# Four patch banks, direct loads of the rest weights, throw-away matmuls, and scatter rows normalised in their own chunk

## Chip, core and metric

One core of a Trainium2 chip runs the whole program. The metric is the device time in microseconds of one execution. Matrix products run on TensorE (PE; PEld is its weight load), element work on VectorE (DVE), ScalarE (ACT) and GpSimd (POOL); SyncE (SP) only issues DMAs.

## What is computed

32 images of 3x96x96 are cut into 6x6 patches of 16 pixels, with four copies shifted by 8 pixels: 36 patches of 3840 features. They are layer-normed and projected to 192 features, and 128 text tokens are appended: 164 tokens a batch. Then, with `ln` for a layer norm without weights,

```
xn = (patches - mu) * rsqrt(var + 1e-5) * ln_gamma + ln_beta;  h = concat(xn @ W.T + b, txt)
x  = ln(h);  k, v, gate = of batch 0 alone;  q of every batch
fw(t+1) = 0.95 * fw(t) + 0.1 * gate(t) * outer(k(t), v(t));  r(t) = q(t) @ fw(t)
h  = h + x + r @ w_out.T
x  = ln(h);  xf = rms_norm(x) * norm_w;  probs = softmax(xf @ router_w.T)
y  = sum over the top 2 of 8 experts e:  probs[e] * (silu(xf @ g[e].T) * (xf @ u[e].T)) @ d[e].T
out = h + x + y
```

## The kernel before

**Layout.** Four tokens of all 32 batches make a tile of 128 rows: 41 tiles, of which 9 hold patch tokens. `hres` holds all of them. The recurrence is rewritten in chunks of 16 tokens (4 tiles, 11 chunks, the last of one tile): a chunk reads a state for what lies in the past and a masked score matrix for the present.

**Patches.** `patch(p)` (nine, L687) does 24 matmuls into bank `p % 2` and waits for the read-out of patch p-2. On ScalarE `squares(p + 1)` sums squares of an image band, then the root of patch p is taken; there are two band buffers, so bands 2 and 3 are loaded when the squares of their predecessors are done (L380). On VectorE `patch_out(p)` (L1003) forms the variance, reads the bank into `tmp`, waits for the root and writes the tokens. Between them lie the text tiles' statistics (`stats1`, `scale1`) and normalisation (`add_norm`).

**Between.** Behind the last patch, TensorE projects keys and values of batch 0 (`project`, L719), multiplies them by query and output weights (`text_kv`, L728), picks batch 0's patch tokens with selection matrices (L766 to L769), computes gates (L776), repeats the projections for the first 48 tokens and multiplies those (`head_kv`, L739). ScalarE copies the keys out, VectorE the values (`vals`, L1091).

**Attention, chunk c.** Each engine runs its own list in order; semaphores join them. TensorE (L849): `turn(c+1, 0)` transposes two tiles of the next chunk into bank 1; `past` and `present` of tiles 0 and 1; `turn(c+1, 1)`, which needs bank 1 read out; `past` and `present` of tiles 2 and 3; `state`, `rows(c+2)`, `scores(c+1)`. VectorE (L1220): units of weights (`low`), `residual`, router `sums`, top-2 `picks`, `stats_2`, `mask(c+1)`, `places` (the row of each token in its expert's region), `low`, `scale2`. ScalarE:

```
for c in range(CHUNKS):            # L586
    xT_out(c + 1, 0); high(...); xT_out(c + 1, 1)
    norm2(c - 1)                   # waits for scale2(c - 1); writes the scatter rows xf
    state_out(c + 1); high(...); rows(c + 2)
    add_norm2(c - 1); std2(c)      # waits for stats_2(c)
```

GpSimd scatters each tile of `xf` twice to the regions of its two experts in DRAM (`scatter`, L648), eight indirect DMAs a full chunk; there are three `xf` buffers.

**Expert weights.** Each f32 weight is kept as a rounded high part and the remainder. `high(n)` on ScalarE writes the first, `low(n)` on VectorE the second; a `unit` is a fourth of the eight down matrices' block, or a piece of one expert's gate and up weights: the first 128 input rows as one unit, the last 64 as two, staged through a ring of three buffers that SP reloads as they come free (L388 to L393). 28 units are spread over 22 half-chunks by `turn_units`.

**Experts.** When all tokens are counted, SP clears the tails of the regions (L397), VectorE makes a table of 89 slots of 128 rows, and a pipeline over the slots loads rows (L414), transposes them, multiplies, and stores results (L666). A last stage gathers and adds (L1310).

## Time and profile before

| | us |
|---|---|
| median of 3 runs | 653.4 |
| the runs | 644.21, 653.4, 655.39 |
| the profiled execution, its own time | 646.63 |
| its span | 644.8 |
| busy PE / DVE / ACT / POOL | 508.8 / 366.3 / 282.9 / 185.8 |
| granted TensorE clock, mean share | 0.881 |

The span runs from the first to the last instruction; the execution's own time has 1.8 us around it. Busy PE is time with a matmul listed. A granted clock of 1 is 2.4 GHz, 0.5 is 1.2 GHz. "Idle before" is the time that an engine waited just before an instruction and what released it.

### The profile page before, as it was taken

How to read it: one execution, taken by the hardware profiler on the slowest of the kernel's cores; microseconds unless marked ns; L12 is line 12 of the kernel's file. 1: busy time of each engine (PE TensorE's matmuls, PEld its weight loads, DVE VectorE, ACT ScalarE, POOL GpSimd, SP SyncE). 2: the span in 40 equal slices, each digit the busy share in tenths (PEclk: the TensorE clock that was granted, in tenths of full speed). 3: DMA queues.
4: the chain of work that ended last, by engine and by line, in shares of the span. 5: the costliest groups of instructions: out<-in, count | busy, mean ns of one | idle time of the engine just before them, and what ended most of it. 6: DMA issues, size and time to landing. Idle time of an engine off the chain costs nothing.

```text
span 644.8 us, 12710 instructions
## 1 busy us (share of the span) xinstructions
PE 508.8 (79%) x3128; PEld 474.7 (74%) x3129; DVE 366.3 (57%) x1254; ACT 282.9 (44%) x702; POOL 185.8 (29%) x270
## 2 busy tenths in 40 slices
PE   5998689999767837750699999999999999998000
PEld 2897689878555726540699999999999999998000
DVE  3546457217747635576355655666665556655297
ACT  0364673426556516552344444444444444444100
POOL 0000000000736654456033333333333333334100
PEclk9999999659969878765699999999999999999555
DMA  8972022710212322223122222222222222221795
GB/s 361 429 315 98 2 98 88 256 38 1 87 51 87 100 74 68 70 80 112 46 74 74 72 72 72 72 75 75 79 72 72 72 72 72 72 80 45 253 370 140
DMA packets 55579, 71.62 MB, mean 111 GB/s; under 512 B 18961, under 2 KB 50258, under 8 KB 54018
## 3 DMA queue, kind: packets, MB, share of 16 engines
q1 hardware_dynamic: 41408, 48.12, 23.6%
q0 software_dynamic: 8208, 16.95, 7.4%
q10 hardware_dynamic: 5938, 6.26, 2.8%
q8 instruction: 11, 0.18, 0.1%
q14 instruction: 14, 0.11, 0.1%
HBM read 49.43 MB, written 21.86 MB: 111 GB/s over the span
## 4 chain that ended last, share of the span: by engine, by line
PE 56%; DVE 21%; ACT 6%; another core or an unknown queue 5%; DMA 4%; issue 4%; SPq 2%; ACTq 1%; POOL 0%; DVEq 0%; POOLq 0%
PE bank L921 5%; PE bank L917 5%; PE bank L919 5%; PE bank L920 5%; PE bank L918 5%; PE bank L928 4%; DVE hres L1310 4%; PE bank L937 4%; PE pair L937 4%; DMA band<-in_bands 3%; PE pair L906 3%; ACT sqjunk L447 3%; PE pair L822 3%; PE bank L698 2%
## 5 line engine op out<-in xcount | busy, mean ns | idle before, releaser
L654 POOL DMA_INDIRECT disp<-xf,posu x82 | 80.7, 984 | 220.0 <-ACT xf L557 193.8
L666 POOL DMA_INDIRECT ydram<-ysb,dnow x89 | 87.3, 981 | 69.4 <-POOL dnow L663 66.4
L1275 DVE TENSOR_TENSOR hh<-sg,bank 128x384 f32<-128x384 f32 x89 | 49.3, 554 | 95.1 <-ACT sg L614 93.9
L614 ACT ACTIVATE sg<-bank 128x384 f32<-128x384 f32 x89 | 43.7, 491 | 113.2 <-PE bank L921 113.2
L698 PE MATMUL bank<-wcT,imgT 128*128 128x193 f32 x432 | 74.2, 332 | 10.8 <-DVE tmp L1015 10.8
L698 PEld LDWEIGHTS bank<-wcT,imgT 128*128 128x128 f32 x432 | 72.2, 192 | 12.3 <-DVE tmp L1015 7.7
L917 PE MATMUL bank<-wa,xh 128*128 x178 | 68.1, 383 | 0.0
L919 PE MATMUL bank<-wa,xl 128*128 x178 | 60.5, 340 | 0.0
L921 PE MATMUL bank<-wa,xl 128*128 x178 | 60.5, 340 | 0.0
L920 PE MATMUL bank<-wa,xh 128*128 x178 | 60.5, 340 | 0.0
L918 PE MATMUL bank<-wa,xh 128*128 x178 | 60.1, 338 | 0.0
L822 PE MATMUL pair<-nst,xT 96*128 96x208 f32 x164 | 44.1, 399 | 19.7 <-ACT nst L537 9.7
L663 POOL COPY dnow<-dest 128x1 uint32 (+1 forms) x89 | 16.5, 186 | 123.0 <-DVE ysb L1285 123.0
L822 PEld LDWEIGHTS pair<-nst,xT 96*128 96x128 f32 x164 | 34.3, 227 | 21.6 <-ACT nst L537 10.1
L1278 DVE TENSOR_TENSOR htl<-bank,hth 128x384 fp32r<-128x384 f32 x89 | 49.0, 550 | 0.9 <-ACT hth L617 0.9
L906 PE MATMUL pair<-ident,xs 128*128 128x128 f32 x178 | 34.8, 277 | 18.6 <-DMA xs<-disp 18.6
L937 PE MATMUL pair<-wd,hth 128*128 x135 | 44.8, 381 | 0.4 <-DVE htl L1278 0.4
L928 PE MATMUL bank<-ident,hh 128*128 128x128 f32 x267 | 43.6, 272 | 0.6 <-DVE htl L1278 0.6
L937 PE MATMUL bank<-wd,hth 128*128 x132 | 43.8, 381 | 0.0
L617 ACT CAST hth<-bank 128x384 fp32r<-128x384 f32 x89 | 42.4, 476 | 0.8 <-PE bank L928 0.8
L826 PE MATMUL pair<-crow,sm 128*128 128x200 f32 x82 | 26.6, 412 | 19.8 <-DVE sm L1122 16.2
L611 ACT CAST xh<-pair 128x256 fp32r<-128x256 f32 x89 | 33.4, 376 | 17.4 <-PE pair L906 17.0
(228 smaller groups left out, 1112.8 us busy)
## 6 DMA issues: line engine op xcount, KB each, us to landing
xs<-disp SPq DMA_DIRECT2D x89, 96.0 KB, 2.0
imgT<-in_pixels SPq DMA_DIRECT2D x4, 1536.0 KB, 18.1
band<-in_bands SPq DMA_DIRECT2D x4, 1536.0 KB, 13.0
yall<-ydram SPq DMA_DIRECT2D x5, 768.0 KB, 13.7
yall<-ydram ACTq DMA_DIRECT2D x5, 768.0 KB, 14.8
hres<-in_text SPq DMA_DIRECT2D x1, 3072.0 KB, 34.0
wa<-in_gate_up_w SPq DMA_DIRECT2D x8, 384.0 KB, 8.8
ring<-in_gate_up_w SPq DMA_DIRECT2D x32, 96.0 KB
```

The lines of the kernel that those rows point to most:

```text
L654: pool.indirect_dma_start(disp, bass.IndirectOffsetOnAxis(ap=posu[c % XBUF][:, 2 * j + k:2 * j + k + 1], axis=0), xfd[c % XBUF][:, j, :], None
L666: pool.indirect_dma_start(ydram, bass.IndirectOffsetOnAxis(ap=dnow[b][:], axis=0), ysb[b][:], None).then_inc(s_ys[b], 16)
L698: ins = pe.matmul(bank[p % 2][:, 0:193], imgT[:, 2 * i + dr, j + s, c, :], wcT[:, k, :], start=(k == 0), stop=(k == 23))
L822: pe.matmul(o, xT[c % 2][:, m, P * j:P * j + P], nst[c % 2][:, m, :], start=(m == 0), stop=False)
L906: ins = pe.transpose(bank[5][:, P * m:P * m + P], xs[b][:, P * m:P * m + P], ident[:])
L917: pe.matmul(acc, xh[o][:, 0:P], high, start=True, stop=False)
L918: pe.matmul(acc, xh[o][:, 0:P], low, start=False, stop=False)
L919: pe.matmul(acc, xl[o][:, 0:P], high, start=False, stop=False)
L920: pe.matmul(acc, xh[o][:, P:2 * P], rest, start=False, stop=False)
L921: ins = pe.matmul(acc, xl[o][:, P:2 * P], rest, start=False, stop=True)
L928: ins = pe.transpose(bank[4][:, P * c:P * c + P], hh[b][:, P * c:P * c + P], ident[:])
L937: pe.matmul(bank[6 + o][:, 0:2 * D], hth[o][:, P * c:P * c + P], wd[:, both], start=(c == 0), stop=False)
```

## The change

Seven edits. Patches use four banks, so a patch waits for the read-out of the fourth one back; the root is taken ahead of the next squares, and the normalisation of patch p-1 follows the read-out of patch p. The projections for the text move ahead of patch 8, all `text_kv` of the values ahead of the selection, and ScalarE copies the values too. `warm(n)`, n bf16 matmuls of 512 columns of ones into bank 3 that nobody reads, stands in nine places: 76 calls in all. The rest weights are loaded straight into their final place, and the ring is gone; an expert's rest is one unit (20 units in all), and its high part takes two passes of 768 columns on 64 rows. The down weights' four units move into the patch stage (p = 5, 6). Loads change order on the SP queue. `norm2(c)` is called at the end of iteration c on ScalarE instead of in the middle of iteration c+1.

```diff
+LATE = (3, 4, 7, 8)
...
-UNITS = DOWN_UNITS + 3 * NE
-RING = 3
+UNITS = DOWN_UNITS + 2 * NE
+PATCH_BANK = (0, 1, 5, 6)
+PROJ_BANK = (4, 7, 2, 3)
...
-        ring = [at(f"ring{i}", [P, DE], F32, r_gh + 18688 + 1536 * i) for i in range(RING)]
+        rest = at("rest", [P, 2, DE], F32R, r_gh + 18688)
...
+            return None if k < 0 else (k // 2, k % 2)
...
-            return range(t * UNITS // TURNS, (t + 1) * UNITS // TURNS)
+            n = UNITS - DOWN_UNITS
+            return range(DOWN_UNITS + t * n // TURNS, DOWN_UNITS + (t + 1) * n // TURNS)
...
+            sp.dma_start(hres3[:, PTILES:TILES, :], text).then_inc(s_txt, 16)
             sp.dma_start(imgT[:, 4:6], pixels[:, 4:6]).then_inc(s_img[2], 16)
-            sp.dma_start(hres3[:, PTILES:TILES, :], text).then_inc(s_txt, 16)
...
+            sp.dma_start(aw[:], attn_w).then_inc(s_attw, 16)
+            sp.wait_ge(s_sq, 12)
+            sp.dma_start(band[0][:], bands[:, 2]).then_inc(s_band[2], 16)
             sp.dma_start(imgT[:, 6:8], pixels[:, 6:8]).then_inc(s_img[3], 16)
-            sp.dma_start(aw[:], attn_w).then_inc(s_attw, 16)
-            for i in range(2):
-                sp.wait_ge(s_sq, 12 + 9 * i)
-                sp.dma_start(band[i][:], bands[:, 2 + i]).then_inc(s_band[2 + i], 16)
-
+            sp.dma_start(wd4[:, :, 1, :].bitcast(F32), down_w).then_inc(s_rawd, 16)
+
+            def load_expert(e):
+                sp.dma_start(wa5[:, e, 1].bitcast(F32), gu_w[0:P, e]).then_inc(s_rawe[e], 16)
+                for half in range(2):
+                    sp.dma_start(wa5[64 * half:64 * half + 64, e, 2].bitcast(F32), gu_w[P:D, e]).then_inc(s_rawe[e], 16)
+
+            sp.wait_ge(s_sq, 21)
+            sp.dma_start(band[1][:], bands[:, 3]).then_inc(s_band[3], 16)
+            sp.wait_ge(s_pat, 6)
+            for e in range(2):
+                load_expert(e)
+            sp.wait_ge(s_pat, PTILES)
             sp.wait_ge(s_sq, 30)
-            sp.wait_ge(s_pat, PTILES)
-            sp.dma_start(wd4[:, :, 1, :].bitcast(F32), down_w).then_inc(s_rawd, 16)
...
-            sp.wait_ge(s_kv, 4 * NH)
-            for r in range(2 * NE):
-                if r >= RING:
-                    sp.wait_ge(s_lo, DOWN_UNITS + 3 * ((r - RING) // 2) + (r - RING) % 2 + 2)
...
-                    sp.dma_start(ring[r % RING][64 * half:64 * half + 64, :], gu_w[P:D, r // 2, r % 2]).then_inc(s_rawr[r % RING], 16)
+            for e in range(2, NE):
+                load_expert(e)
...
+                        if e:
+                            act.wait_ge(s_lo, n - 1)
+                        nc.scalar.activation(rest[64:P], wa5[64:P, e, 2].bitcast(F32), ACT.Copy, scale=nwab[64:P, 1:2])
+                        both = wa5[0:64, e, 2]
+                        ins = nc.scalar.activation(both, both.bitcast(F32), ACT.Copy, scale=nwab[0:64, 1:2])
+                ins.then_inc(s_hi, 1)
...
+                act.wait_ge(s_pv, p + 1)
+                nc.scalar.activation(sd2[:, p:p + 1], sd2[:, 16 + p:17 + p], ACT.Sqrt).then_inc(s_psd, 1)
                 if p + 1 < 9:
                     squares(p + 1)
-                act.wait_ge(s_pv, p + 1)
-                nc.scalar.activation(sd2[:, p:p + 1], sd2[:, 16 + p:17 + p], ACT.Sqrt).then_inc(s_psd, 1)
...
-                if p == 5:
+                if p == 4:
                     act.wait_ge(s_v0, 1)
                     nc.scalar.activation(sx[:, 0:1], mv0[:, 1:2], ACT.Sqrt, bias=cst[:, C_EPS:C_EPS + 1]).then_inc(s_sd0, 1)
...
+                if p in (5, 6):
+                    for n in (2 * p - 10, 2 * p - 9):
+                        high(n)
+                if p == 7:
+                    for n in range(4):
+                        projection(n)
...
+            for h in range(NH):
                 act.wait_ge(s_kv, h + 1)
-                nc.scalar.copy(keysT[:, :, 2:CHUNKS, CHUNK * seat(h):CHUNK * seat(h) + CHUNK],
...
-            for n in range(4):
-                projection(n)
+                text_out(keysT, h, s_kvout)
             std_text(4)
             for h in range(NH):
-                keys(h)
+                act.wait_ge(s_kv, NH + h + 1)
+                text_out(valsT, h, s_vtout)
             act.wait_ge(s_pick, 1)
             add_norm(4)
...
-                if c:
-                    norm2(c - 1)
...
                 std2(c)
-            norm2(CHUNKS - 1)
+                norm2(c)
...
+            def warm(n):
+                for _ in range(n):
+                    pe.matmul(bank[3][:], onesb[:], onesb[:].unsqueeze(1).to_broadcast([P, 4, P]), start=True, stop=True)
...
-                if p >= 2:
-                    pe.wait_ge(s_patout, p - 1)
+                if p >= 4:
+                    pe.wait_ge(s_patout, p - 3)
...
-                    ins = pe.matmul(bank[p % 2][:, 0:193], imgT[:, 2 * i + dr, j + s, c, :], wcT[:, k, :],
+                    ins = pe.matmul(bank[PATCH_BANK[p % 4]][:, 0:193], imgT[:, 2 * i + dr, j + s, c, :], wcT[:, k, :],
...
-                    pe.wait_ge((s_kvout, s_vvout)[which], 2 * hp - 2)
+                    pe.wait_ge((s_kvout, s_vtout)[which], 2 * hp - 2)
...
+            for p in range(1, 7):
+                patch(p)
+            pe.wait_ge(s_x0n, 1)
+            for m in range(2):
+                ins = pe.transpose(bank[2][0:DH, P * m:P * m + P], x0n[:, DH * m:DH * m + DH], ident[:])
+            ins.then_inc(s_x0t, 1)
+            patch(7)
             pe.wait_ge(s_attw, 16)
             pe.wait_ge(s_x0T, 1)
             for n in range(4):
                 w = SPAD - TEXT0
                 for k in range(2):
-                    ins = project(bank[4 + n][:, w * k:w * k + w], (wkT, wvT)[n // 2], 2 * (n % 2) + k, TEXT0, SPAD)
+                    ins = project(bank[PROJ_BANK[n]][:, w * k:w * k + w], (wkT, wvT)[n // 2], 2 * (n % 2) + k, TEXT0, SPAD)
                 ins.then_inc(s_k0, 1)
+            patch(8)
+            pe.wait_ge(s_patout, 8)
             pe.wait_ge(s_wqc, 1)
-            for hp in range(4):
-                if hp < 2:
-                    pe.wait_ge(s_k0out, 2 * hp + 2)
-                text_kv(0, hp)
+            pe.wait_ge(s_k0out, 4)
+            for which in range(2):
+                for hp in range(4):
+                    text_kv(which, hp)
...
+                    if n % 3 == 2:
+                        warm(1)
             ins.then_inc(s_pick, 1)
-            for hp in range(4):
...
-                text_kv(1, hp)
+            warm(2)
+            pe.wait_ge(s_head, 1)
+            for m in range(2):
+                ins = pe.matmul(bank[3][:, 0:SPAD], wgR[:, m, :], x0T[:, m, :], start=(m == 0), stop=(m == 1))
+            ins.then_inc(s_g8, 1)
...
-                pe.wait_ge(s_vvout, 6 + 2 * which)
+                pe.wait_ge(s_vtout, 6 + 2 * which)
...
+            pe.wait_ge(s_gs, 1)
+            warm(2)
...
                 for hp in range(4):
                     head_kv(which, hp)
+                    warm(1)
...
+                warm(1)
...
+                warm(1)
                 pe.wait_ge(s_sm, c + 1)
...
+                    warm(1)
...
+                    warm(1)
...
+            warm(16)
...
-                acc = bank[p % 2]
-                mean, var, q, rs = (sd2[:, 25 + k:26 + k] for k in range(4))
+                acc = bank[PATCH_BANK[p % 4]]
...
+            def patch_norm(p):
+                i, j = p // 3, p % 3
+                t, inv = tmp[p % 2], sd2[:, 28 + p % 2:29 + p % 2]
                 v.wait_ge(s_patout, p + 1)
                 v.wait_ge(s_psd, p + 1)
-                st.link(v.reciprocal(rs, sd2[:, p:p + 1]))
+                st.link(v.reciprocal(inv, sd2[:, p:p + 1]))
...
+                    a, raw, top = (0, wa5[:, e, 1], wa5[:, e, 0]) if k == 0 else (64, wa5[64:P, e, 2], rest[64:P])
+                    ins = v.scalar_tensor_tensor(out=raw, in0=raw.bitcast(F32), scalar=nwab[a:P, k:k + 1],
+                                                 in1=top.bitcast(F32), op0=ALU.mult, op1=ALU.subtract)
...
             for p in range(9):
                 patch_out(p)
+                if p:
+                    patch_norm(p - 1)
...
+                if p in (5, 6):
+                    for n in (2 * p - 10, 2 * p - 9):
+                        low(n)
+                if p == 6:
                     v.wait_ge(s_ptok, 6)
                     st.mark(bn1(EARLY, 0))
-                if p == 7:
...
+            patch_norm(8)
...
-            for h in range(4):
-                vals(h)
...
+            v.wait_ge(s_k0, 5)
+            v.tensor_copy(k0T[:, :, 0:HEAD_S], bank[4][:, 0:4 * HEAD_S].rearrange("p (k s) -> p k s", k=4)).then_inc(s_k0head, 1)
```

`high`, `low` and `projection` are otherwise moved unchanged; in the old attention wait, `s_vvout` counted the values' ten copies, and now `s_vtout` counts the eight of the text.

## Rows read from the trace of the kernel before

**Rows 1.** Page, chain of waits: shares of the span by engine.

```profile
PE 56%; DVE 21%; ACT 6%; another core or an unknown queue 5%; DMA 4%; issue 4%; SPq 2%; ACTq 1%; POOL 0%; DVEq 0%; POOLq 0%
```

**Rows 2.** Page, group of the patch matmuls; then the last patch in the timeline.

```profile
L698 PE MATMUL bank<-wcT,imgT 128*128 128x193 f32 x432 | 74.2, 332 | 10.8 <-DVE tmp L1015 10.8
...
98.40 8.12 PE L698 MATMUL bank<-wcT,imgT 128*128 128x193 f32 x48
```

**Rows 3.** Timeline, VectorE and ScalarE in a patch cycle: start us, us, line, operation [idle before].

```profile
71.81 0.16 DVE L1019 RECIPROCAL sd<-sd 128x1 f32<-128x1 f32 x1 [5.39 <-ACT sd L479]
...
73.72 2.18 DVE L1031 BATCH_NORM_STATS2 stats<-hres 128x6 f32<-128x192 f32 x8
...
65.10 3.61 ACT L472 ACTIVATE hres<-hres,lt 128x192 f32<-128x192 f32 x8
```

**Rows 4.** Band loads: time from issue to landing.

```profile
DMA to landing us min/median/max: 6.3/13.0/22.4
```

**Rows 5.** Timeline, VectorE: the selection matrices are ready.

```profile
112.60 0.19 DVE L1089 TENSOR_TENSOR selr<-cst,lt 128x36 f32<-128x36 f32 x1
```

**Rows 6.** Timeline, TensorE, from the selection to the first scores.

```profile
113.79 1.67 PE L769 MATMUL bank<-selr,hres 128*96 128x4 f32 x18
...
118.22 0.55 PE L736 MATMUL bank<-v0T,aw 64*96 64x144 f32 x1
...
120.39 1.54 PE L776 MATMUL bank<-x0T,qpar 96*128 96x176 f32 x4
...
123.83 1.99 PE L721 MATMUL bank<-x0T,aw 96*128 96x48 f32 x16 [0.42 <-DVE valsT L1093]
...
138.29 3.76 PE L816 MATMUL bank<-xT,keysT 96*128 96x512 f32 x4
```

**Rows 7.** Stretch: length, busy us of PE, PEld, DVE, ACT, POOL, PEclk, DMA share, GB/s.

```profile
126.00:146.00 20.00, 19.24 (x117) 16.37 (x117) 2.54 (x6) 6.58 (x13) 0.00 (x0) 0.50 0.10 31
```

**Rows 8.** Timeline, residuals: second pair of chunk 0, the one tile of chunk 10.

```profile
150.09 0.74 DVE L1132 SCALAR_TENSOR_TENSOR hres<-pair,lt,hres 128x192 f32<-128x192 f32 x2 [1.79 <-PE pair L826]
...
289.13 0.41 DVE L1132 SCALAR_TENSOR_TENSOR hres<-pair,lt,hres 128x192 f32<-128x192 f32 x1
```

**Rows 9.** Timeline, chunk 1: VectorE, then ScalarE, then TensorE.

```profile
157.71 0.16 DVE L1198 SCALAR_TENSOR_TENSOR bb<-mv,rs 128x8 f32<-128x8 f32 x1
...
159.18 1.47 DVE L1132 SCALAR_TENSOR_TENSOR hres<-pair,lt,hres 128x192 f32<-128x192 f32 x4
...
155.49 0.56 ACT L517 COPY xT<-bank 96x512 f32<-96x512 f32 x1
...
158.49 1.86 ACT L557 ACTIVATE xf<-hres,bb,rs 128x192 f32<-128x192 f32 x4
...
157.18 0.60 PE L796 MATMUL bank<-ident,hres 128*96 128x128 f32 x4
```

**Rows 10.** Groups, 140 to 300 us: count, busy us, mean ns of one.

```profile
L1211 DVE SCALAR_TENSOR_TENSOR wa<-wa,qpar 128x768 fp32r<-128x768 f32 x8 | 8.1, 1015 | 1.2 <-ACT wa L576 0.9
...
L1206 DVE TENSOR_TENSOR wd<-wd 128x1152 fp32r<-128x1152 f32 x4 | 5.4, 1354 | 3.2 <-ACT wd L571 3.2
...
L832 PE MATMUL pair<-ecs,onesb 128*128 128x32 bf16 (+1 forms) x11 | 2.0, 178 | 0.0
```

**Rows 11.** Page, group of the scatter DMAs.

```profile
L654 POOL DMA_INDIRECT disp<-xf,posu x82 | 80.7, 984 | 220.0 <-ACT xf L557 193.8
```

**Rows 12.** Chain of waits in order of time: start us, us, what.

```profile
170.06 2.91 another core or an unknown queue
...
178.43 4.54 another core or an unknown queue
...
223.81 11.25 another core or an unknown queue
```

**Rows 13.** Timeline, from the last chunk to the experts.

```profile
300.82 0.19 DVE L1258 CAST tab<-slotf 128x91 int32<-128x91 f32 x1
...
312.31 0.67 PE L917 MATMUL bank<-wa,xh 128*128 x1
```

108 lines of the change are left out of this document (36 added, 72 removed).

## The prediction

> **What bounds the kernel now.** I read the chain of waits first: 56% of the span is TensorE, 21% VectorE, and 5% (about 31 us of the 644.8) is ended by "another core or an unknown queue" on a kernel that runs on one core [rows 1]. Most of TensorE's share is the expert stage, 310 to 590 us, which the change leaves alone. So the question is the first 310 us, which fall into three stages with different limits.
>
> In the patch stage the reader is to see a ping-pong: TensorE's 432 matmul records cost 74.2 us and it idles only 10.8 us for a bank [rows 2], while VectorE waits 5.39 us in one patch for a root that ScalarE issues behind the squares of the next patch [rows 3]. Between the last patch and the first scores TensorE works on small matmuls, and for 20 us it has them at a granted clock of 0.50, the 1.2 GHz level [rows 7]. In the attention stage a bare cycle is 9.83 us (second residual pair of chunk 0 at 150.09, that of chunk 1 at 159.18 + 0.74 = 159.92), but chunk 0 to chunk 10 takes 139.0 us, 13.9 a chunk [rows 8, 9]. Of the 40.7 us above ten bare cycles, the unknown waits are about 31; the longest, 11.25 us, falls while scatter rows of two chunks follow each other without a gap, and so do those of 2.91 and 4.54 [rows 12]. GpSimd itself is busy 80.7 us with 82 scatters, about 1.26 us apart, 10.1 us for a full chunk [rows 11]; it idles for rows that ScalarE has not normalised.
>
> **The change, part by part.**
>
> **Patches.** Four banks remove the 10.8 us of bank waits [rows 2]. Root before squares, and the normalisation of patch p-1 behind the read-out of patch p, remove the 5.39 us wait; what is left on VectorE is 1.9 for the normalisation (71.81 to 73.72) plus statistics and scales, on ScalarE 3.61 for the text rows and 3.1 for squares and root (68.71 to 71.81), both under TensorE's 8.12 a patch [rows 2, 3]. Late next is the fourth band. It is asked for when the squares of patch 5 end; at 8.1 a patch that is about 67, and it lands 6.3 us later at best [rows 4], near 74. Then come squares 3.1, two down-weight units on ScalarE and their two halves on VectorE of 1.35 each [rows 10], in front of the read-out of patch 6, and two more in front of the copy of the first batch's transpose. That copy is ready near 91; patch 7 has ended near 86. TensorE waits about 5 us there; its new wait for the read-out of patch 7 is long met. The projections (32 records, twice the 16 that take 1.99 [rows 6], so 4.0) now stand before patch 8: last patch ends at 91 + 4 + 8.1 = 103, against 98.40 + 8.12 = 106.5. Behind it stood 6.3 us to the selection matrices, ready at 112.79 [rows 5]; now the normalisation of patch 7 is in between too, 1.9. So 111.2, a gain of 1.6. Without the 5 us wait it is 6.6; with a band or weights later, a loss of 3. The reordered loads cost nothing beyond that: the text goes ahead of pixels that are first needed at patch 3, the pixels of the last row are needed at patch 6, some 20 us after their new place, and the SP queue has nothing else due while it waits for squares.
>
> The value copies move to ScalarE behind the root of the last statistics, which is queued in front of them and waits for the patch tokens; TensorE's third value pair waits for it. The selection therefore starts about 1.5 earlier, not 1.6.
>
> **Between.** From 118.22 to 123.83 lay value products and the 1.54 of the gate; with the values ahead, 5.6 shrinks to about 1.9: a gain of 3.7 [rows 6]. Added on the path are 16 throw-away matmuls (six in the selection, two behind the gate sums, eight among the head products; two more hide behind the head copy). No row shows their shape. 
>
> The Trainium skill ("TensorE: Matmul & The Clock Gate", Part 1, What's actually happening) says that the throttled state is the default and that activity releases it; by it a TensorE that mostly waits stays at the low level, and the sum would be 4 us higher. The trace agrees in so far as the half clock lasts from 126 to 146 with TensorE listed busy 19.24 us of 20, on small products [rows 7].
>
> **Attention.** Here an edit with a price hides in the order of ScalarE's queue. `norm2(c)` moves to the end of its own iteration. There it waits for `scale2(c)` of VectorE, and queued behind it is `xT_out(c+2, 0)`. TensorE needs that copy in `turn(c+2, 1)`, which stands between the first and the second pair of chunk c+1. Today the copy starts at 155.49, long before the turn at 157.18 [rows 9]. After: the scales of chunk 0 were ready at 157.71 + 0.16 = 157.87 with one 1.35 unit before them; on average 0.74 us of the new units (8 of 11 such places, 1.015 each) stand there [rows 10], so 157.27; `norm2` 0.1 + 2.05 (four of 1.86 in all and two small copies); the copy 0.56, a signal 0.1; turn and second pair 157.18 to 159.92, so 2.74; the throw-away in front of `past(c, 2)` 0.25. Second residual pair at 163.07 instead of 159.92 [rows 9]: 3.15 a chunk, in the eight chunks 1 to 8 that have such a turn. The other three throw-aways of a chunk lie in waits for the state, the mask or the next chunk. Eight cycles of 13.0 and two of 9.83 give 123.6 bare, 15.4 under today's 139.0.
>
> On top come the unknown waits. 18.7 of the 31 us fell in double bursts of scatters [rows 12]. With 10.1 us of scatters in a cycle of 13, bursts do not join, so I leave those out and keep what lone bursts had: about 12 over six chunks, 2.0 each, nine times 18. The rest of today's excess, 9.7, was units and low clock: eight units fewer, four of 1.35 gone early; I take none. 123.6 + 18 = 141.6: **+2.6**. Bounds: none of the waits, -15.4; all 40.7 kept, +25.3. `norm2(c)` also needs the scatters of chunk c-3 landed, two cycles after their burst: met. The earlier scatters themselves end nothing: the path runs through VectorE and TensorE to the counts. Rest rows cost ScalarE two passes of 768 instead of two of 384, inside its idle time; if that cover goes, 8 x 0.9 = 7, inside the upper bound. The 32 ring loads leave the SP queue; nobody waited for them in the chain.
>
> **Towards the experts.** 16 throw-aways start when the table is ready, 301.01, and end by 308, before the first expert rows reach TensorE (experts' first product 312.31 [rows 13]): hidden; if the gap closed they would cost up to 7. They may lift the clock of the first products: between nothing and 2.5; I take 1.5.
>
> **Sum.** -1.5 - 2.1 + 2.6 - 1.5 = -2.5 on the profiled execution's own 646.6 (span 644.8 and 1.8 around it): 644.1, a ratio of 0.996. That execution is 1% under the median of 653.4, inside 644.2 to 655.4; the median scales to **651**.
>
> **The rivals.** *Slower:* the unknown waits stay. One begins inside a scatter burst and now hits TensorE's turn and second pair, since these follow `norm2` and so the burst's start; all 40.7 us of excess come on top of cycles of 13. +25.3 there, -1 in front, 0 at the end: 671, as median 678. It decides from an average excess of 3 us a chunk up (I have 2.0). For it: every long unknown wait lies in a burst. Against: the longest two lay in joined bursts. Chance 0.17.
>
> *Faster:* the waits came from joined bursts and from expert loads running beside them, and vanish; the clock stays up. -15.4, patch stage without its 5 us -6.4, between -6, end -2.5: 616; more likely half of the first stage, 620, as median 626. For it: the change spreads the bursts and empties the queue. Against: lone bursts had waits too. Chance 0.28.
>
> *The clock does not answer:* TensorE stays at 0.50 between the last patch and the scores although the throw-aways are there, as it did with products in every gap [rows 7]; they cost their low-level price, 16 x 0.45 = 7.2, and give nothing, nor at the end: +7.1 on the forecast, 651, as median 658. Chance 0.13. It is the case that the rule of the Trainium skill named above points to.
>
> **How the numbers follow.** Forecast 0.42, median 651. A measurement of this kernel can tell about 2%, so faster is under 640 and slower over 666.5. Faster: the second rival 0.28 and 0.05 of the forecast's own spread: 0.33. Slower: 0.16 of the first rival and 0.03 of the others: 0.19. Same: 0.48. The range 623 to 672 leaves out about half of each outer rival.
>
> **What would show it.** Right: no bank wait over 1 us before patch 7, a TensorE wait near 86 us for the transpose copy; `turn(c+2, 1)` starting only after ScalarE's four rows of chunk c, second pairs 13 us apart; GpSimd with a gap in every chunk; value products ahead of the selection. Wrong: second pairs 10 us apart, granted clock near 1 from 115 to 146, or unknown waits of over 5 us in single bursts.

## The result, and the profile after

The change made the kernel slower: 667.0 us (median of 6 runs, 665.1 to 669.6) against 644.0 (6 runs, 634.6 to 655.4), ratio 1.042 with an interval of 1.034 to 1.050. The profiled execution took 669.55, span 667.8, which is 23.0 over the 644.8 of before. Medians here stand over all runs; ratios leave disturbed runs out, among them one of 2851.59 us in e9 and one of 1791.4 in e11.

Read by the kernel's own milestones, the 23 us come from every stretch but the last:

| stretch | before | after | difference |
|---|---|---|---|
| start to selection | 113.59 | 116.22 | +2.6 |
| selection to first turn of chunk 0 | 20.6 | 28.7 | +8.1 |
| first turn to second residual pair of chunk 0 | 15.9 | 17.6 | +1.7 |
| second residual pair of chunk 0 to the tile of chunk 10 | 139.0 | 147.8 | +8.8 |
| chunk 10 to the experts' first product | 23.2 | 25.6 | +2.5 |
| experts to the end | 332.5 | 331.9 | -0.6 |

The page after, chain of waits, answers [rows 1]: the unknown queue falls from 5% to 0%, and ScalarE's share rises from 6% to 11%.

```profile
PE 53%; DVE 18%; ACT 11%; issue 7%; DMA 6%; SPq 2%; ACTq 1%; POOL 0%; another core or an unknown queue 0%; DVEq 0%; POOLq 0%
```

The selection starts with its first product (L766 before, L781 after); [rows 6] begins with the one behind it, at 113.79.

**Patch stage.** Timeline after, TensorE, then VectorE and ScalarE (start us, us, engine, line, operation, in brackets the idle time before it and what ended it). It answers [rows 2, 3].

```profile
77.13 8.04 PE L712 MATMUL pair<-wcT,imgT 128*128 128x193 f32 x48
91.85 7.08 PE L727 MATMUL bank<-x0T,aw 96*128 96x144 f32 x32 [6.68 <-DVE x0T L1125]
98.76 1.48 PE L712 MATMUL bank<-wcT,imgT 128*128 128x193 f32 x8
...
86.73 2.63 DVE L1087 TENSOR_TENSOR wd<-wd 128x1152 fp32r<-128x1152 f32 x2 [2.11 <-ACT wd L477]
91.13 0.57 DVE L1125 COPY x0T<-bank 96x256 f32<-96x256 f32 x1
...
85.54 2.21 ACT L477 CAST wd<-wd 128x1152 fp32r<-128x1152 f32 x2
```

No bank wait is left among TensorE's waits from 30 to 115 us. In their place TensorE stands 6.68 us ahead of the projections, for a copy that VectorE issues behind two halves of the down-weight units, which waited for ScalarE. The projections then take 7.08 us.

**Selection to heads.** Timeline after, TensorE; then the stretch that answers [rows 7] (length, busy us of each engine, granted clock, DMA share, GB/s).

```profile
116.22 0.53 PE L781 MATMUL bank<-selr,onesf 128*96 128x36 f32 x2
...
117.52 0.59 PE L699 MATMUL bank<-onesb 128*128 128x512 bf16 x1
117.90 1.01 PE L784 MATMUL bank<-selr,hres 128*96 128x4 f32 x6
...
126.51 3.49 PE L727 MATMUL bank<-x0T,aw 96*128 96x48 f32 x16
...
134.19 0.39 PE L750 MATMUL bank<-k0T,aw 64*96 64x48 f32 x1
...
135.01 0.61 PE L699 MATMUL bank<-onesb 128*128 128x512 bf16 x1
135.55 0.39 PE L750 MATMUL bank<-k0T,aw 64*96 64x48 f32 x1
...
144.48 0.61 PE L699 MATMUL bank<-onesb 128*128 128x512 bf16 x1
144.88 1.06 PE L814 MATMUL bank<-ident,hres 128*96 128x128 f32 x4
```

```profile
130.00:145.00 15.00, 15.00 (x91) 10.16 (x92) 1.21 (x4) 0.85 (x2) 0.00 (x0) 0.50 0.00 1
```

A throw-away product holds TensorE for 0.38 us in the selection (117.52 to 117.90), at a granted clock of 0.50, 1.2 GHz. Among the head products it costs more: a group with its throw-away product takes 1.36 us (134.19 to 135.55), in e2, without them and at the same level, about 0.65. The clock doesn't move although TensorE is listed busy for 15.00 of 15.00 us.

**Loop.** Timeline after: second residual pair of chunk 0, then ScalarE and TensorE behind it, then chunk 10. It answers [rows 8, 9].

```profile
162.46 0.74 DVE L1170 SCALAR_TENSOR_TENSOR hres<-pair,lt,hres 128x192 f32<-128x192 f32 x2 [2.00 <-PE pair L844]
...
168.02 0.28 ACT L573 ACTIVATE sq<-mv,cst 128x4 f32<-128x4 f32 x1
170.28 0.20 ACT L582 COPY xf<-cst 128x8 f32<-128x8 f32 x1 [1.98 <-DVE bb L1236]
...
170.48 1.87 ACT L586 ACTIVATE xf<-hres,bb,rs 128x192 f32<-128x192 f32 x4
172.25 0.57 ACT L546 COPY xT<-bank 96x512 f32<-96x512 f32 x1
...
172.96 1.06 PE L814 MATMUL bank<-ident,hres 128*96 128x128 f32 x4 [2.90 <-ACT xT L546]
...
310.29 0.41 DVE L1170 SCALAR_TENSOR_TENSOR hres<-pair,lt,hres 128x192 f32<-128x192 f32 x1
```

This is the order that the prediction described: rows, then the copy, then the turn on TensorE. The waits of the same stretch (engine, line, waited for: us in total, times, longest) say how often; "remote" is the unknown releaser. First after, then before.

```profile
PE bank L814 <- ACT xT L546: 19.7, 8, 3.1
...
ACT xf L582 <- DVE bb L1236: 15.1, 9, 2.4
...
ACT crow L560 <- remote: 7.7, 4, 2.5
...
DVE sm L1160 <- remote: 2.1, 3, 0.8
```

```profile
ACT xT L517 <- remote: 17.4, 4, 5.2
...
ACT nst L537 <- remote: 15.6, 2, 12.9
DVE hres L1132 <- remote: 14.2, 2, 11.3
DVE ohm L1182 <- remote: 12.1, 3, 5.0
...
ACT crow L531 <- remote: 7.5, 1, 7.5
...
DVE sm L1122 <- remote: 4.6, 1, 4.6
```

Waits for the unknown releaser fall from 71.4 us, summed over engines, to 9.8. The kernel lost them and its loop still grew by 8.8 us.

**Towards the experts.** Timeline after, TensorE; it answers [rows 13].

```profile
325.49 5.79 PE L699 MATMUL bank<-onesb 128*128 128x512 bf16 x16 [11.49 <-DVE tab L1279]
...
335.92 0.67 PE L940 MATMUL bank<-wa,xh 128*128 x1
336.38 0.52 PE L941 MATMUL bank<-wa,xh 128*128 x1
```

The experts' products at 336 us take 0.52 us, at the lower clock: it rose under the sixteen throw-away products and was down again when the experts' rows were there (stretches after, granted clock behind the five engines).

```profile
330.00:333.40 3.40, 1.28 (x6) 0.39 (x4) 0.00 (x0) 0.00 (x0) 0.00 (x0) 0.99 0.20 45
333.40:340.00 6.60, 5.08 (x17) 4.41 (x18) 1.29 (x4) 2.53 (x5) 0.00 (x0) 0.50 0.27 63
```

### The profile page after: what moved, and what is told of

It is laid out like the page before. It is cut to its first block, busy times and chain, and to the rows that moved or that the text cites. A ratio compares the mean times of both kernels' runs of the same rounds, so it can differ in the third digit from the quotient of the medians.

```text
span 667.8 us, 12837 instructions
## 1 busy us (share of the span) xinstructions
PE 540.4 (81%) x3204; PEld 493.5 (74%) x3205; DVE 361.4 (54%) x1239; ACT 293.6 (44%) x709; POOL 186.4 (28%) x270
## 4 chain that ended last, share of the span: by engine, by line
PE 53%; DVE 18%; ACT 11%; issue 7%; DMA 6%; SPq 2%; ACTq 1%; POOL 0%; another core or an unknown queue 0%; DVEq 0%; POOLq 0%
DMA band<-in_bands 6%; PE bank L944 5%; PE bank L940 5%; PE bank L943 5%; PE bank L942 5%; PE bank L941 5%; PE bank L951 4%; DVE hres L1331 4%; ACT sqjunk L452 4%; PE bank L960 4%; PE pair L960 4%; PE pair L929 3%; ACT xf L586 2%; DVE wa L1091 2%; DVE stats L1184 2%
## 5 line engine op out<-in xcount | busy, mean ns | idle before, releaser
L940 PE MATMUL bank<-wa,xh 128*128 x178 | 68.1, 383 | 0.0
L840 PE MATMUL pair<-nst,xT 96*128 96x208 f32 x164 | 47.2, 422 | 0.0
L621 ACT CAST xh<-pair 128x256 fp32r<-128x256 f32 x89 | 33.7, 378 | 26.4 <-PE pair L929 19.5
L699 PE MATMUL bank<-onesb 128*128 128x512 bf16 x76 | 34.0, 494 | 11.5 <-DVE tab L1279 11.5
L840 PEld LDWEIGHTS pair<-nst,xT 96*128 96x128 f32 x164 | 39.4, 246 | 2.1 <-ACT nst L566 0.2
L712 PE MATMUL bank<-wcT,imgT 128*128 128x193 f32 x240 | 40.2, 327 | 0.2 <-DVE zrow L995 0.2
L712 PEld LDWEIGHTS bank<-wcT,imgT 128*128 128x128 f32 x240 | 39.3, 189 | 0.6 <-DVE zrow L995 0.6
L844 PE MATMUL pair<-crow,sm 128*128 128x200 f32 x82 | 28.0, 432 | 12.7 <-DVE sm L1160 12.7
## 6 DMA issues: line engine op xcount, KB each, us to landing
imgT<-in_pixels SPq DMA_DIRECT2D x4, 1536.0 KB, 14.9
```

The source lines that it names most:

```text
L712: ins = pe.matmul(bank[PATCH_BANK[p % 4]][:, 0:193], imgT[:, 2 * i + dr, j + s, c, :], wcT[:, k, :], start=(k == 0), stop=(k == 23))
L840: pe.matmul(o, xT[c % 2][:, m, P * j:P * j + P], nst[c % 2][:, m, :], start=(m == 0), stop=False)
L940: pe.matmul(acc, xh[o][:, 0:P], high, start=True, stop=False)
```

## The experiments

Kernels of one set ran on one chip, beside runs of the kernel before: the first two sets on one chip, each of the others on a chip of its own. The chip of the first comparison is not on record. Each kernel has one trace, and the time marks in the tables are of that one. Starts in these tables count the weight load, up to 0.4 us ahead of the product. "Stretch" is the time from chunk 0's second residual pair to chunk 10's tile, "middle" that from the selection's start to chunk 0's first turn.

### First set: each suspect alone

**e1_norm_late.** The rows go back to their old place.

```diff
+                if c:
+                    norm2(c - 1)
                 if c + 1 < CHUNKS:
                     state_out(c + 1)
...
-                norm2(c)
+            norm2(CHUNKS - 1)
             add_norm2(CHUNKS - 1)
```

> The changed kernel with one part undone: chunk c-1's scatter rows are normalised in chunk c again, ahead of the copy of the state. Theory A (the place of the rows on ScalarE lengthens the loop): the stretch from the second residual pair of chunk 0 to that of chunk 10 falls from 147.8 to about 139 us, the kernel gains about 9 us on the changed one (ratio to the kernel before about 1.028 in place of 1.042). Rival B (the place of the rows is free; what it costs TensorE it gives back by taking the single waits of 3 to 11 us for an unknown releaser out): these waits come back in the trace, the stretch stays at 146 to 150 us, the ratio at 1.04. Rival C (the loop is longer through the throw-away products in it alone): stretch and ratio as in the changed kernel, and the waits for an unknown releaser stay away.

**e2_no_throwaway.** Every `warm(...)` call of the changed kernel is deleted.

```diff
-                    if n % 3 == 2:
-                        warm(1)
...
-            warm(2)
...
-            warm(16)
```

> The changed kernel without any throw-away product (selection, gate, heads, loop, ahead of the experts). Theory A (they cost their time at half clock and don't raise it): first turn of chunk 0 comes 6 to 8 us earlier after the selection's start, the loop is 2 to 4 us shorter, in all 8 to 12 us less than the changed kernel (ratio to the kernel before about 1.028). Rival D (they hold the clock up in the loop, at a price in the middle): the middle gains 6 us, the loop loses 6 or more by a lower clock, ratio still about 1.04; granted clock of the whole run falls from 0.867 to 0.85 or less. Rival E (they cost nothing, being in waits): nothing moves by more than 2 us.

**e3_both_undone.** Both edits together.

> The changed kernel without throw-away products and with the scatter rows in their old place; what is left of the change are the four patch banks, the weights loaded without the ring, the values' copies on ScalarE and the down units in patches 5 and 6. Theory A: the two gains add, about 649 us where the kernel before takes 644 (ratio about 1.008), and what is left over is the later start of the selection (116.2 against 113.8). Rival F (the rest of the change costs too, through the values' copies on ScalarE or the weights' loads in the patch stage): ratio 1.02 or more.

**e4_before_norm_own.** The kernel before with `norm2(c)` behind `std2(c)`, in place of `norm2(c - 1)` ahead of `state_out(c + 1)`.

> The kernel before with one part of the change alone: each chunk's scatter rows are normalised at its own end on ScalarE. Theory A: the second turn of the next chunk comes after them, the bare cycle goes from 9.8 to 13 us, the waits for an unknown releaser partly vanish, the stretch from chunk 0's to chunk 10's second residual pair goes from 139 to 145 to 150 us, ratio 1.01 to 1.02. Rival B (free exchange): 139 us and ratio 1.00. Rival G (the scatters spread out help): stretch under 135 us, ratio under 0.99.

Measured:

| kernel | median us | ratio to before | selection at | middle | stretch |
|---|---|---|---|---|---|
| before, its first profile | 644.0 | 1 | 113.6 | 20.6 | 139.0 |
| after | 667.0 | 1.042 [1.034, 1.050] | 116.2 | 28.3 | 147.8 |
| e1 | 657.0 | 1.019 [1.010, 1.028] | 114.6 | 28.3 | 136.3 |
| e2 | 658.0 | 1.020 [1.011, 1.029] | 115.4 | 20.3 | 149.0 |
| e3 | 652.8 | 1.014 [1.003, 1.025] | 114.6 | 20.3 | 142.4 |
| e4 | 662.9 | 1.027 [1.016, 1.039] | 116.5 | 16.5 | 156.4 |

The rows' place costs 11.5 us of stretch in the changed kernel (147.8 against 136.3) and 17.4 in the kernel before (156.4 against 139.0): theories B, C and G fall. The waits for the unknown releaser do come back in e1, 68.1 us from 134 to 320, as B had it, and the loop is shorter all the same. Without throw-away products the same edit is worth less, 6.6 us of stretch (e2 against e3), with overlapping ratios. The throw-away products of the middle cost 8 us (28.3 against 20.3) and D and E fall there. Eighteen stand there, the sixteen of the prediction and the two that it has behind the head copy. e4's middle of 16.5 has no throw-away product and the same code as the 20.6 of before: the old order's middle spreads from 16.5 to 22.4 over its six traces, that of the changed kernel without them is 20.0 to 20.3 in nine. With both undone something is left over, 0.3 to 2.5%: F is not excluded.

Where the cycle's length comes from is read in e2, whose clock is full when the cycle starts. Timeline, chunk 0 to chunk 1: VectorE, ScalarE, TensorE, and the next second pair.

```profile
152.72 0.74 DVE L1160 SCALAR_TENSOR_TENSOR hres<-pair,lt,hres 128x192 f32<-128x192 f32 x2 [1.94 <-PE pair L839]
...
159.13 1.01 DVE L1081 SCALAR_TENSOR_TENSOR wa<-wa,qpar 128x768 fp32r<-128x768 f32 x1
...
160.56 0.20 ACT L582 COPY xf<-cst 128x8 f32<-128x8 f32 x1 [1.99 <-DVE bb L1226]
...
159.83 0.50 PE L839 MATMUL pair<-crow,sm 128*128 128x200 f32 x2
163.23 1.06 PE L809 MATMUL bank<-ident,hres 128*96 128x128 f32 x4 [2.89 <-ACT xT L546]
...
167.94 0.74 DVE L1160 SCALAR_TENSOR_TENSOR hres<-pair,lt,hres 128x192 f32<-128x192 f32 x2 [1.06 <-PE pair L839]
```

The granted clock in the same stretch (the number after the five engines):

```profile
156.00:160.00 4.00, 2.39 (x16) 2.21 (x15) 3.76 (x15) 1.02 (x3) 0.00 (x0) 1.00 0.00 0
160.00:163.20 3.20, 0.33 (x2) 0.03 (x2) 0.49 (x4) 2.62 (x8) 0.98 (x1) 0.57 0.01 3
163.20:168.00 4.80, 4.77 (x18) 4.69 (x19) 1.83 (x4) 2.24 (x3) 3.58 (x5) 0.58 0.26 85
```

The wait of 2.89 us is not all of the price. The clock fell to half at 160.42, just as the wait began, so this wait didn't bring the fall; behind it the clock is 0.58 in the mean, the turn takes 1.06 us where [rows 9] has 0.60, and from the turn to the second pair pass 4.7 us (163.23 to 167.94) where [rows 9] gave 2.7. The cycle is 15.2, not 13.0.

### Second set: the middle, the units, the order of the copy

**e5_late_loop_only** is e1 without the throw-away products between the selection and the heads.

> The changed kernel with the scatter rows in their old place and without the throw-away products of the middle (selection, gate, heads); those of the loop and the 16 ahead of the experts stay. Differs from e3_both_undone in these alone. Theory A (throw-away products in the loop hide in waits and do nothing): as e3_both_undone, 650 to 655 us (ratio 1.005 to 1.018), stretch between the second residual pairs of chunks 0 and 10 at 136 to 143 us. Rival D (they hold the clock up in the loop; e1_norm_late's loop of 136.3 against e3_both_undone's 142.4 is that): about 647, ratio 1.00. Rival H (they cost in the loop once the rows are late): over 656.

**e6_units_in_loop** is e5 with the down-weight units back among the loop's units.

```diff
-            n = UNITS - DOWN_UNITS
-            return range(DOWN_UNITS + t * n // TURNS, DOWN_UNITS + (t + 1) * n // TURNS)
+            return range(t * UNITS // TURNS, (t + 1) * UNITS // TURNS)
...
-                if p in (5, 6):
-                    for n in (2 * p - 10, 2 * p - 9):
-                        high(n)
```

> As e5_late_loop_only, and the four down-weight units leave patches 5 and 6 and are done in the loop among the others, as in the kernel before. Theory P (these units keep VectorE from the copy of the transposed tokens: TensorE's wait of 6.7 us at 91.85, and with it the projections at half clock): that wait falls under 3 us, the selection starts at 110 to 113 us in place of 114.7 to 116.3, the loop grows by 1 to 3 us, the kernel gains 0 to 3 us on e5_late_loop_only. Rival Q (late bands set the patch stage): the wait goes and the selection still starts at 114 or later.

**e7_copy_ahead** is the changed kernel without the middle's throw-away products, and with the copy ahead of the rows.

```diff
-                if c + 1 < CHUNKS:
-                    xT_out(c + 1, 0)
+                if c == 0:
+                    xT_out(1, 0)
...
                 std2(c)
+                if c + 2 < CHUNKS:
+                    xT_out(c + 2, 0)
                 norm2(c)
```

> The changed kernel without the throw-away products of the middle, the scatter rows at their own chunk's end, and one step moved: ScalarE copies the first transposed half of chunk c+2 ahead of chunk c's scatter rows and not behind them. Theory A (the rows' place costs because that copy, which the second turn on TensorE needs, stands behind them): TensorE's waits for that copy (20.5 us in 9 pieces in the changed kernel) fall under 6 us, and the stretch from chunk 0's to chunk 10's second residual pair falls from 148 to 135 to 140 us; 646 to 651 us, ratio 0.995 to 1.01. Rival R (the loop with the rows at the end is bound by ScalarE's whole work of a chunk, or by the contention of the scatters, not by that copy): the waits for the copy go and the stretch stays at 146 to 150 us; 657 to 660 us.

**e8_twice_middle** is the changed kernel with `warm(2)` for each `warm(1)` and `warm(4)` for each `warm(2)` of the middle.

> The changed kernel with twice as many throw-away products in the middle (32 in place of 16; loop and end as in the changed kernel). Theory A (each costs its time at half clock): from the selection's start to chunk 0's first turn 28.3 becomes about 36 us (the 16 cost 8.0, by e2_no_throwaway's 20.3), and the kernel takes 673 to 676 us, ratio about 1.05. Rival I (only too few: with more of them the clock rises to full before the heads): granted clock 1 somewhere between 115 and 145 us, the stretch 30 us or less, ratio 1.04 or less.

| kernel | median us | ratio to before | selection at | middle | stretch |
|---|---|---|---|---|---|
| e5 | 648.5 | 1.010 [1.002, 1.017] | 114.6 | 20.3 | 139.6 |
| e6 | 641.8 | 1.003 [0.998, 1.009] | 105.6 | 20.0 | 139.7 |
| e7 | 649.7 | 1.020 [1.012, 1.028] | 114.7 | 20.3 | 143.1 |
| e8 | 666.3 | 1.044 [1.027, 1.060] | 115.5 | 27.7 | 147.0 |

e5 comes out just under the span that theory A gave it and over D's: the ratios of e3 and e5 overlap, and the loop's throw-away products can't be told from nothing. Those of the middle can: 28.3 against 20.3 once more, and 8.5 us of time against e1.

e6: theory P holds. With the units out of the patches the selection starts 9 us earlier, at 105.6 and not the 110 to 113 expected, and the kernel gains 6.7 us on e5. Timeline, TensorE, e6; then the same row of e5:

```profile
76.89 8.04 PE L710 MATMUL pair<-wcT,imgT 128*128 128x193 f32 x48
84.77 4.08 PE L725 MATMUL bank<-x0T,aw 96*128 96x144 f32 x32
88.69 8.04 PE L710 MATMUL bank<-wcT,imgT 128*128 128x193 f32 x48
```

```profile
90.22 6.72 PE L729 MATMUL bank<-x0T,aw 96*128 96x144 f32 x32 [4.89 <-DVE x0T L1122]
```

There is no wait, and the projections take 4.08 us and not 6.72: the wait cost its 4.9 us and 2.6 more in what stood behind it. The loop took the four units for nothing here (139.7 against 139.6).

e7: theory A's mechanism holds, with less gain than it expected. TensorE's waits for the copy fall from 19.7 us to 2.1 and the stretch by 4.7, not by 8 to 13. ScalarE now waits for VectorE's statistics (24.6 us in 8 pieces) and VectorE for ScalarE's weight units.

e8: mostly rival I. Its clock and its middle came in the trace, its ratio of 1.04 or less did not quite (1.044), and theory A's 36 us did not come. The eighteen more cost nothing in the traced run, since the clock rose in the middle of the heads: granted clock 0.51 from 115 to 130 and 0.89 from 130 to 145, where the changed kernel has 0.50. The middle was 27.7 us and chunk 0's first half 11.3 where it had been 18.0. Two of four runs took 661 to 662 us, two 671 to 672; the mean granted clock of these two is 0.877 and 0.870, against 0.890 and 0.894, so it may not have risen in them; they have no trace. Denser throw-away products can lift the clock here; what they bring is at most what they cost.

```profile
115.00:130.00 15.00, 15.00 (x72) 11.10 (x68) 0.77 (x3) 5.31 (x14) 0.00 (x0) 0.51 0.75 182
130.00:145.00 15.00, 14.24 (x119) 8.71 (x118) 2.34 (x7) 2.67 (x5) 0.00 (x0) 0.89 0.00 1
```

### Third set: repairs, and the banks alone

**e9_units_and_copy** joins e6's and e7's edits (rows at their own chunk's end).

> The changed kernel with the repairs that the runs point to together: no throw-away products in the middle, the down-weight units in the loop (as e6_units_in_loop), the rows at their chunk's end but the copy of the first transposed half ahead of them (as e7_copy_ahead). If the repairs add: selection's start at 105 to 107 us (e6), stretch between second residual pairs 143 to 146 us (e7's 143.1, and four units more in the loop), 640 to 644 us, ratio to the kernel before 0.99 to 1.00. Rival: the rows in their old place stay better, since the loop with them at the end is bound by ScalarE's wait for VectorE (24.6 us before the roots in e7_copy_ahead): 645 us or more, above e6_units_in_loop's 641.8.

**e10_scales_first** is e2, and on VectorE:

```diff
                 places(c)
+                scale2(c)
                 for n in turn_units(2 * c + 1):
                     low(n)
-                scale2(c)
```

> e2_no_throwaway (rows at their chunk's end, no throw-away products) with one step moved: VectorE works out a chunk's scales ahead of the weight units of the chunk's second half, not behind them. Theory A (the cycle grew by 5 us and not by the 3.15 of the prediction, since ScalarE, once the rows are at the end, waits 2 us for the scales behind a weight unit, 160.56 in e2_no_throwaway, and the copy and TensorE's second turn wait with it): cycles of the first chunks 13 to 14 us in place of 15.2, stretch 149 falls to 138 to 143 us, kernel 648 to 653 in place of 658. Rival J (the unit behind them is late instead and holds the next mask or residual): stretch 147 to 150 us, 656 to 660.

**e11_all_reordered** is e9 with e10's edit.

> e9_units_and_copy with the scales ahead of the weight units too. With the copy already ahead of the rows TensorE doesn't wait for them, so theory A expects little: stretch 1 to 4 us shorter than in e9_units_and_copy, 637 to 643 us, ratio 0.985 to 0.998. Rival J as in e10_scales_first: the same or up to 3 us more.

**e12_before_four_banks** is the kernel before with the banks and what they need:

```diff
-                if p >= 2:
-                    pe.wait_ge(s_patout, p - 1)
+                if p >= 4:
+                    pe.wait_ge(s_patout, p - 3)
...
-                    ins = pe.matmul(bank[p % 2][:, 0:193], imgT[:, 2 * i + dr, j + s, c, :], wcT[:, k, :],
+                    ins = pe.matmul(bank[PATCH_BANK[p % 4]][:, 0:193], imgT[:, 2 * i + dr, j + s, c, :], wcT[:, k, :],
...
                 patch_out(p)
+                if p:
+                    patch_norm(p - 1)
```

> The kernel before with one part of the change alone: four patch banks, VectorE's normalising of a patch one patch later, and the root ahead of the squares on ScalarE; the order on TensorE, the loads, the values' copies and all of the loop as before. Theory P (the banks are worth what e6_units_in_loop shows once nothing spoils them): selection starts at 105 to 108 us in place of 113.8, ratio 0.98 to 0.99. Rival K (the 8 us of e6_units_in_loop come from the order of the loads and from the projections ahead of patch 8): selection at 111 to 114 us, ratio 0.995 to 1.005.

| kernel | median us | ratio to before | selection at | middle | stretch |
|---|---|---|---|---|---|
| e9 | 644.2 | 1.002 [0.998, 1.005] | 106.4 | 20.3 | 142.0 |
| e10 | 649.8 | 1.012 [1.007, 1.018] | 114.6 | 20.3 | 140.9 |
| e11 | 638.0 | 0.983 [0.973, 0.993] | 106.3 | 20.3 | 135.2 |
| e12 | 636.7 | 0.985 [0.976, 0.994] | 103.7 | 19.5 | 139.4 |

e10: theory A holds. ScalarE's wait for the scales falls from 1.99 us to 1.06 in chunk 0, the turn comes at 160.58 (9.6 us behind the second pair, in e2 10.5), and the stretch is 8 us shorter. e9 only ties with e6, the rival's half: the rows at the end bring nothing while the scales stand behind a unit. With the scales ahead as well (e11) the kernel gains 6 us on e9, and 6.8 us of stretch, more than the 1 to 4 expected.

e12: theory P holds and K falls. The banks, with the order of root and normalisation that they need, give 10 us; the reordered loads and projections of the changed kernel are not needed for it. In e12 TensorE runs patches 5 to 8 without a pause and the projections behind them at 93.72 in 4.08 us. It beats both kernels.

### Fourth set: on another chip

**e13_banks_and_loop** is e12 with the loop's order of e11. **e14_only_units_undone** is the changed kernel with e6's edit alone. **e15_reordered_no_throwaway** is e11 without any `warm`.

> e12_before_four_banks (ring, old order on TensorE, old loads, no throw-away products) with the loop's order as e11_all_reordered has it: rows at their own chunk's end, the copy of the first transposed half and the chunk's scales ahead of them. Theory A (order alone sets what the rows at the end cost): stretch 139.4 falls to 133 to 138 us, as 149.0 fell to 135.2 on the changed kernel's side; 630 to 636 us, ratio 0.97 to 0.985. Rival L (with the ring's twelve more units in the loop ScalarE and VectorE are full: the rows at the end cost 156.4 in e4_before_norm_own against 149.0 in e2_no_throwaway): stretch 142 us or more, 640 us or more.

> The changed kernel with one part undone: the four down-weight units go back from patches 5 and 6 into the loop; throw-away products and the rows' place stay as changed. Theory P (these units alone turned the patch stage's gain into a loss): selection starts at 105 to 107 us in place of 116.3, the rest stays (28 us to the first turn, loop 148 to 151), 657 to 661 us. Rival Q (the gain in e6_units_in_loop was given in part by a warmer clock in the middle or is lost behind the throw-away products): selection early and the kernel over 663.

> e11_all_reordered without the throw-away products of the loop and the 16 ahead of the experts: none are left. Theory A (in the loop they lie in waits and neither cost nor bring anything): stretch 134 to 137 us (e11: 135.2), 636 to 640 us. Rival D (they hold the clock up in the loop): granted clock between chunk 0 and chunk 10 lower by 0.05 or more and stretch 139 us or more, 642 or more. Rival H (they cost): stretch 132 or less, 633 or less.

| kernel | median us | ratio to before | selection at | middle | stretch |
|---|---|---|---|---|---|
| before, in this set | 611.0 | 1 | | | |
| e13 | 613.5 | 1.003 [0.998, 1.009] | 105.3 | 22.2 | 113.3 |
| e14 | 654.8 | 1.075 [1.066, 1.084] | 106.6 | 28.3 | 146.9 |
| e15 | 615.6 | 1.011 [1.002, 1.019] | 106.1 | 20.3 | 117.1 |

The kernel before took 604 to 613 us in this set and 635 to 655 in the earlier ones. e14 confirms the units in the changed kernel itself: the selection starts at 106.6 in place of 116.2. In none of the three profiles does a completion signal of TensorE come more than 1 us after the end of its product, as it does 34 times in the first profile of the kernel before, and the two reordered loops fell to 113 and 117. So e15 can't be held against e11, nor e13 against e12. The last set was made for what this opened.

### Fifth set: without the late signals

Nothing is edited: **e16_before_again** is the kernel before, **e17_after_again** the changed one, **e18_banks_again** is e12.

> The kernel before, unchanged, for a profile of it on another chip. In the comparison runs beside e13 to e15 it took 604 to 613 us, 35 less than beside all runs before these, and in those three profiles no signal of a TensorE product comes more than 1 us after its end, while the first profile of before has 29 that come 3 to 20 us late between 140 and 310 us. Theory U (the waits for an unknown releaser are these late signals, and they go with the chip): if the run takes about 610 us, none is late, the cycles are 9.8 to 11 us and the stretch 100 to 112; if it takes about 645, they are there and the stretch is 135 to 145. Rival V (the 35 us lie elsewhere, in the experts or the last stage): about 610 us with a stretch over 125 us.

> The changed kernel, unchanged, on the same chip as e16_before_again. Theory U: it had hardly any such waits to lose, so where before takes 610 it takes 655 to 668 (ratio about 1.08 to 1.09, e14_only_units_undone having 1.075 with the patch stage repaired), cycles of 14 to 16 us as ever; where before takes 645, ratio about 1.04. Rival V: it gains 30 us as well, ratio 1.04 on any chip.

> e12_before_four_banks, unchanged, on the same chip. The patch stage has nothing to do with the late signals: 8 to 10 us faster than before on any chip, ratio 0.98 to 0.99; about 600 us where before takes 610. Rival: with the late signals gone the loop waits for something else that the early start doesn't move, ratio 0.995 to 1.005.

| kernel | median us | ratio to before | selection at | middle | stretch |
|---|---|---|---|---|---|
| e16 | 608.8 | 1.000 [0.995, 1.005] | 115.2 | 18.9 | 98.5 |
| e17 | 653.9 | 1.073 [1.065, 1.081] | 114.6 | 28.3 | 140.1 |
| e18 | 601.6 | 0.986 [0.980, 0.992] | 103.2 | 22.4 | 97.0 |

Theory U holds and V falls: where the late signals are missing the 35 us are missing, and they are missing in the loop. The chain of waits of e16 has no unknown queue, and its second pair of chunk 0 and tile of chunk 10 are 98.5 us apart:

```profile
PE 59%; DVE 21%; ACT 6%; DMA 5%; issue 4%; POOL 2%; ACTq 1%; SPq 1%; DVEq 0%; POOLq 0%
```

```profile
147.90 0.74 DVE L1132 SCALAR_TENSOR_TENSOR hres<-pair,lt,hres 128x192 f32<-128x192 f32 x2 [0.89 <-PE pair L826]
...
246.44 0.41 DVE L1132 SCALAR_TENSOR_TENSOR hres<-pair,lt,hres 128x192 f32<-128x192 f32 x1
```

That is ten cycles of 9.85 in the mean, the bare cycle of the prediction. The changed kernel there has a stretch of 140.1: its loop costs 41.6 us on this chip. In the first comparison the kernel before had 40.5 us more (139.0 less 98.5) and the changed one 7.7 more (147.8 less 140.1), so the change seemed to cost 8.8. How the 41.6 divide isn't shown: e1 to e4 have no twins without late signals.

For e13 this decides against theory A: 113.3 is 16 us over e18's 97.0 with the same banks, on two chips that both lack the late signals and on which the kernel before takes 611.0 and 609.0. So the rows at their own chunk's end cost even in the better order, by L's mechanism or another. e11's ratio of 0.983, equal to e12's, comes from a chip with late signals, where the old order's loop is 40 us longer; e15, which has e11's loop without throw-away products, has 1.011. Of what ran without late signals only e12's edit pays.

The same comparison takes back what e6 gave. e14 starts its selection 8.0 us before e17 (106.6 against 114.6), its loop is 6.8 us longer (146.9 against 140.1), and the ratios are the same, 1.075 and 1.073. Without late signals moving the four units earns nothing in the changed kernel.

The traces say a little more of the late signals than their number. All fourteen traces that have them (before, after, e1 to e12) lack most of the landing records of the scatters: 269 to 534 of 1312 are there, against 1292 to 1312 in e13 to e18. And in all fourteen the late ones lie between the first and the last scatter, none before and none in the experts' stage.

## Why the prediction was wrong

It forecast -2.5 us on the profiled execution and had +23. The late signals carry over into the sizes, but every stage but the last failed on its own.

**Patches: -1.5 forecast, +2.6 measured.** The mechanism was right: no bank wait, and TensorE waits for the transpose copy behind the down-weight units. I sized that wait at 5 us; it was 6.7. What I left out stands behind it: the 32 records of projections, priced at the full-clock 4.0 us, took 7.08 at the lower clock. The two together are 9.8 us, about what taking the units out gives back (116.2 to 106.6 in e14). The part that I took for worth 6.6 us makes the selection start 10 to 12 us earlier alone (e12, e18). The size of +2.6 is loose: the same two kernels have 115.2 (e16) and 114.6 (e17), where the change gains 0.6.

**Between: -2.1 forecast, +8.1 measured.** This is the largest failure, in all three of its terms. The throw-away products cost 8.0 us (28.3 against 20.3, e2) and not 5.6: 0.50 for each of the sixteen that I counted on the path. In the selection one held 0.38, near my 0.35; among the heads it was 0.7. The clock stayed at 0.50 throughout, as in the rival "the clock does not answer". The 4 us of clock did not come. The 3.7 us of the value products moved ahead did not come either: without throw-away products the middle is 20.3, against 20.6 before (18.9 in e16), at a granted clock of 0.50 from 115 to 145 us where before had 0.66 and 0.55 in the first two thirds. The Trainium skill ("TensorE: Matmul & The Clock Gate", Part 1, What's actually happening) has the throttled state as the default that activity releases; the trace agrees in e8, where twice as many products raised the clock, and bounds it in the changed kernel, where a TensorE listed busy 15.00 of 15.00 us stayed at half. The prediction drew from the rule that the 4 us might not come, from a TensorE that mostly waits; they didn't come to one that was busy.

**Attention: +2.6 forecast, +10.5 measured (1.7 to the second pair of chunk 0, 8.8 behind it).** The order was right in each step, rows, copy, turn. Two terms were mis-sized, in opposite directions. The bare cycle was put at 13.0 and is 14.9 in the mean of e17's first eight. In e2's first cycle, 2.2 us over 13.0, the turn comes 10.5 us behind the second pair where I had 10.0 (a whole unit stands ahead of the scales, for the 0.74 us that I took on average), and the next second pair 4.7 behind the turn where I had 3.0: that 1.7 is the low clock under the products behind the wait. I priced a delay and no low clock. That waits bring the low clock on isn't shown for one cycle; the loops as a whole fit it. From 156 to 296 us e17 has a granted clock of 0.87 with TensorE busy 108.71 of 139.70 us, e16 from 142 to 244 us has 0.98 with 86.70 of 102.20. In e2's first cycle the clock had fallen as the wait began, behind a wait of 1.61 us that e3 has too (154.73) and in which e3's clock stayed full. The unknown waits were put at 18 us and came to about 8 (147.8 less e17's 140.1). The bare excess of e17 over my 123.6 is 16.5 us; the two errors together leave 6.2. The 9.7 us that I wrote off as "units and low clock" of the kernel before go with the late signals too, since e16 has ten bare cycles in the mean with the same units.

**Towards the experts: -1.5 forecast, +2.5 measured, and -0.6 behind it.** From chunk 10's tile to the experts' first product the traces spread from 21.2 us (e17) to 28.5 (e8) with the sixteen and from 21.9 (e13) to 28.2 (e18) without, so the 2.5 is no effect of the change that these runs can show. That the sixteen are hidden may be right. The clock gain of 1.5 did not come in the changed kernel's first trace, where the clock was back at the lower level when the experts' products began. It did come in e8, e14 and e17: there the clock was up when they began (e17's below), and from the experts' first product to the end of the span took 330.2 to 330.9 us, against 331.1 to 333.0 in all other traces.

```profile
321.34 0.43 PE L940 MATMUL bank<-wa,xh 128*128 x1
321.62 0.34 PE L941 MATMUL bank<-wa,xh 128*128 x1
```

The rival *slower* had 671 for the profiled execution, and 669.55 was measured. That is luck: its mechanism was that the unknown waits stay, and they fell from 71.4 to 9.8 us.

Of the signs listed as "what would show it", the order of the turn, the gaps of the scatters and the values ahead of the selection were right. "Second pairs 13 us apart" was wrong, by its size.

What stays open: why TensorE's completion signals come late in some traces and not in others. Chip and hour changed together, so neither is shown to be the cause. The missing records leave room for a third, that recording the scatters' landings holds up the signals; every time here comes with a recorded clock, so no run shows what the kernel takes without a recording. Open too is how much of the loop's 41.6 us each edit costs without late signals, and whether single throw-away products in the loop do anything.

## What to carry to other kernels

Price a wait on TensorE also with half clock for what stands behind it: here products behind a wait of 2.9 us took 1.7 more, and behind one of 6.7 us 3.1 more. The loop's throw-away products stood behind the wait in TensorE's queue and didn't cover it: it is 2.90 us with them and 2.89 without (e2). Before moving a step to the end of its own iteration, list what is queued behind it on its engine and move the copy that another engine needs ahead of it. And a wait that the profile gives to nobody may belong to the chip, the hour or the recording and not to the kernel: profile a second chip before carrying it through a sum.
